# A fused adaLN block on one core: first-layer expert products issued in pairs on TensorE

## What is computed

```
h = layernorm(x) * (1 + ca) + sa
q, k, v = h @ Wq.T + bq, h @ Wk.T + bk, h @ Wv.T + bv      # 16 heads of 8
q = softmax(q, over the 8 channels of a head);  k = softmax(k, over the tokens)
state = k.T @ v (per head);  out = q @ state
x = x + ga * ((layernorm(out) * ln_g + ln_b) @ Wo.T + bo)
h = layernorm(x) * (1 + cb) + sb
logits = h @ router_w                                       # 8 experts, the top 2 are kept
y = sum over the chosen e: gate_e * (gelu(h @ w_in[e] + b_in[e]) @ w_out[e] + b_out[e])
x = x + gb * y
```

## Time and profile before

| | |
|---|---|
| median of 3 runs | 424.73 us (422.46 to 429.39) |
| the profiled execution | 429.81 us, its span 427.9 us |
| TensorE busy | 385.2 us of the span |
| VectorE, ScalarE, GpSimd busy | 302.7, 294.3, 221.0 us |
| mean granted TensorE clock | 0.954 of full speed |

### The profile page before, as it was taken

How to read it: one execution, slowest core, us unless ns; L and a number is a source line. 1 busy time by engine, 2 the same in 40 slices (tenths; PEclk the granted TensorE clock), 3 DMA queues, 4 the chain that set the end, 5 groups by cost and what they waited for, 6 DMA issues and landing times.

```text
span 427.9 us, 8780 instructions
## 1 busy us (share of the span) xinstructions
PE 385.2 (90%) x2660; PEld 347.4 (81%) x2660; DVE 302.7 (71%) x1080; ACT 294.3 (69%) x518; POOL 221.0 (52%) x222
## 2 busy tenths in 40 slices
PE   4545777999999999999999999999999999999895
PEld 3445575899888888898898988888989989989885
DVE  3576474678778787878887878878787876764631
ACT  3445547685786878695959778687869596776541
POOL 3432516245564747465556556473746555565341
PEclk9968666799999999999999999999999999999999
DMA  6721005042240606061432415050605132324060
GB/s 199 271 87 38 2 27 197 1 149 100 58 167 28 221 25 222 25 190 56 124 123 70 154 40 205 26 221 25 222 25 171 53 119 106 128 98 190 36 221 27
DMA packets 17789, 47.52 MB, mean 111 GB/s; under 512 B 2068, under 2 KB 4967, under 8 KB 17511
## 3 DMA queue, kind: packets, MB, share of 16 engines
q1 hardware_dynamic: 17568, 46.84, 31.6%
q10 hardware_dynamic: 198, 0.41, 0.3%
HBM read 42.76 MB, written 4.48 MB: 110 GB/s over the span
## 4 chain that ended last, share of the span: by engine, by line
PE 52%; DVE 17%; issue 10%; ACT 7%; POOL 4%; ACTq 1%; DVEq 0%; POOLq 0%
PE pY L647 19%; PE pH L635 6%; PE pH L636 5%; PE pH L637 5%; ACT u L468 3%; ACT L468 3%; DVE top L876 3%; PE pC L587 3%; DVE yg L907 2%; DVE qs L802 2%; DVE qmax L798 2%; PE pB L627 1%; DVE qs L793 1%; PE pB L614 1%; DVE lg_cut L882 1%
## 5 line engine op out<-in xcount | busy, mean ns | idle before, releaser
L647 PEld LDWEIGHTS pY<-wout,v 128*128 128x128 f32 x1024 | 126.4, 191 | 5.7
L647 PE MATMUL pY<-wout,v 128*128 128x128 f32 x1024 | 129.4, 275 | 0.0
L468 ACT ACTIVATE u<-pH,cols 128x512 f32<-128x512 f32 x128 | 87.1, 684 | 38.2 <-PE pH L637 38.0
L338 POOL TENSOR_TENSOR v<-u,gate_bc 128x512 f32<-128x512 f32 x48 | 67.0, 1397 | 48.8 <-ACT u L468 33.8
L902 DVE TENSOR_TENSOR v<-u,gate_bc 128x512 f32<-128x512 f32 x80 | 61.1, 766 | 26.9 <-ACT u L468 13.1
L635 PE MATMUL pH<-h_hi,win_hi 128*128 128x512 f32 x128 | 60.0, 469 | 9.4 <-ACT u L468 9.4
L636 PE MATMUL pH<-h_hi,win_lo 128*128 128x512 f32 x128 | 51.2, 400 | 0.0
L637 PE MATMUL pH<-h_lo,win_hi 128*128 128x512 f32 x128 | 50.7, 396 | 0.0
L328 POOL TENSOR_TENSOR rstd_o<-ve_o,neg_half 128x4 f32<-128x4 f32 x16 | 16.3, 1016 | 57.2 <-DVE ve_o L836 57.2
L346 POOL TENSOR_TENSOR h_lo<-h,h_hi 128x512 fp32r<-128x512 f32 x16 | 21.1, 1317 | 41.2 <-ACT h_hi L409 41.2
L436 ACT ACTIVATE eq<-qs 128x512 f32<-128x512 f32 x16 | 10.1, 631 | 38.7 <-DVE qs L802 38.7
(11 more groups left out here) (144 smaller groups left out, 881.9 us busy)
## 6 DMA issues: line engine op xcount, KB each, us to landing
gate_bc<-route_scratch SPq DMA_DIRECT2D x64, 512.0 KB, 5.4
x_all<-in_L_attn_x SPq DMA_DIRECT2D x16, 256.0 KB, 6.7
out<-x_all SPq DMA_DIRECT2D x16, 256.0 KB, 2.0
gates<-gate_scratch SPq DMA_DIRECT2D x1, 2048.0 KB, 6.9
gb_bc<-gb_scratch SPq DMA_DIRECT2D x1, 1024.0 KB, 4.8
win<-in_L_ffn_w_in SPq DMA_DIRECT2D x1, 512.0 KB
wout<-in_L_ffn_w_out SPq DMA_DIRECT2D x1, 512.0 KB
wmod_sb<-in_L_wmod ACTq DMA_DIRECT2D x1, 384.0 KB, 3.5
```

Source lines behind the costliest of these rows:

```text
L338: pool.tensor_tensor(v[:, e % U, :], u[:, e % U, :], gate_bc[:, par, e, :], ALU.mult).then_inc(s["vp_done"], 1)
L468: act.activation(u[:, e % U, :], pH[:, e % 2, :], ACT.Gelu_apprx_tanh, bias=cols[:, e:e + 1]).then_inc(s["gelu_done"], 1)
L647: i = mm(pY[:, t * P:(t + 1) * P], v[:, e % U, t * P:(t + 1) * P], wout[:, e, :], start=False, stop=(e == NE - 1), skip_group_check=True)
```

## The change

Only PE's `step` is changed, and in it only the order. Before, the eight first-layer products of a step stood apart, each with other PE work ahead of it. After, they stand in four pairs (0 and 1, 2 and 3, 4 and 5, 6 and 7), and the other PE work stands in the gaps. What hidden and combine do, which buffers they use and what they wait for is the same; so is the order on every other engine.

```diff
                 if M:
                     hidden(b, par, 0)
+                    hidden(b, par, 1)
                 if A1:
                     hT(b + 3)
                 if A2:
                     state(b + 2)
-                if M:
-                    hidden(b, par, 1)
                 if Y:
                     combine(b - 1, nxt, 5)
                 if B:
                     h2T(b + 1)
-                if M:
-                    hidden(b, par, 2)
                 if Y:
                     combine(b - 1, nxt, 6)
+                if M:
+                    hidden(b, par, 2)
+                    hidden(b, par, 3)
+                if Y:
                     combine(b - 1, nxt, 7)
                 if A1:
                     kT(b + 3)
-                if M:
-                    hidden(b, par, 3)
                 if A2:
                     attend(b + 2)
...
                 if M:
                     hidden(b, par, 4)
+                    hidden(b, par, 5)
...
                 if M:
                     combine(b, par, 0)
-                    hidden(b, par, 5)
                     combine(b, par, 1)
                     hidden(b, par, 6)
+                    hidden(b, par, 7)
                 if B:
                     gate_turn(b + 1)
                 if M:
                     combine(b, par, 2)
                     combine(b, par, 3)
-                    hidden(b, par, 7)
                     combine(b, par, 4)
```

More of the change, by code:

```diff
@@ L664, in step @@
                     h2T(b + 1)
+                if Y:
+                    combine(b - 1, nxt, 6)
                 if M:
                     hidden(b, par, 2)
+                    hidden(b, par, 3)
                 if Y:
-                    combine(b - 1, nxt, 6)
                     combine(b - 1, nxt, 7)
```

## The result

The changed kernel takes 460.5 us in the median (460.36 to 460.99, 4 runs) against 424.97 us before (422.46 to 429.39, 4 runs). The ratio is 1.082, 95% interval 1.077 to 1.087: slower by 8%, twice the 3.8% that was forecast, and 12 us above the upper end of the range. The profiled execution took 460.52 us, its span is 458.5 us. That of the kernel before is the slowest of its four (429.81 us), so the two traces differ by 30.7 us and the medians by 35.5.

The account below looks back on a forecast made before the run. Bound: PE's work from h6 to kT, then the VectorE and ScalarE chain to the next h6. Ten steps at 1.5 us (15.0), +1.6 for the step to b = 12, -0.5 at the start: +16.1 on 424.73, 440.8 us; range 433.5 to 448.5.

Parts of the forecast that it names:

- rival 3: TensorE's clock: 5 us behind h7 at 1.2 GHz, a step 5 us longer, about 495 us; chance 0.04.
- the term for the hold: VectorE's nmr waits for GpSimd's h2_low, so kT's 2.11 us delay lengthens a step by only 1.5 us.
- the 1.2 of the forecast: On GpSimd, h2_low was to move later in the step by some 1.2 to 1.4 us.
- its upper end: Hold between GpSimd's h2_low and VectorE's nmr stays in full: a step grows by 2.11 us, 448 us; chance 0.12.
- The ruler: PE work or a wait ahead of kT lengthens the step in full; behind kT there is slack under 1 us.
- -0.5 us: At b = 0, h3 fills part of kT's 1.71 us wait for h_lo and h7 hardly waits: -0.5 us.

Follow-up runs that it names:

- the run with the four passes: Changed kernel plus four 128x512 TensorE passes, whose results nobody reads, between hidden(6) and hidden(7): 451.64 us, ratio 1.059.

## Why the prediction was wrong, point by point

**Direction and place were right.** h7 waits for gelu 5 behind ln1_apply, 1.14 us by the idle record, and starts 2.10 us after h6 where 2.11 was forecast. h6 waits as well. gateT_evac waits for gate_turn (1.18 us at 217.49). kbmax and kshift swap the hold. Gelu 5 first removes 28 us: the wait of h7 is the main cause, shown by that run and by h7's move alone (+17.8 us).

**The step that failed most is rival 3's rejection.** "The clock stood at 1.00 through every 0.7 us wait, and the idle share stays under half of that of the start" argued from shorter waits to longer ones. The clock fell in eight steps of eleven, each fall held PE at 1.2 GHz for some 3.4 us, and such a step lost some 1.5 us, 12.6 us in all; the run with the four passes shows it by taking that away and leaving the warm step as it is. The rival had also been priced as one lump of 5 us in every step, which made it look unlike anything that could be mixed with the forecast; a smaller price on top of the forecast was the right case, with a far larger chance than 0.04.

**The second is the term for the hold, 1.5 us a step.** A warm step grew by 2.06. In the warm step above the weighing of expert 2 starts 16.89 us after h6, against 14.86 before. These 2.03 are made of four pieces, each rounded: GpSimd's queue starts 1.17 later (the 1.2 of the forecast), h_low is stretched by 0.47, kshift follows kbmax (0.19), and 0.19 more between nmr and the weighing. What causes the last is not shown. The two starts lie 0.26 us apart in the steady steps of every run where kshift takes 0.16, and 0.07 where it is held. The prediction had named the mechanism of the stretch through the rule of the Trainium skill, GPSIMD Engine Reference, section Key points, that instructions with two SBUF inputs and GpSimd contend, and had set the result, 2.11 a step, as its upper end. By the rule the stretch was to be expected: the weighing of expert 7 has two SBUF inputs and h_low newly meets it. The run with that weighing moved agrees, 1.28 us against 1.74. I kept the rule as a bound where the order already showed who would meet whom. Between kT of b = 1 and of b = 12 that run takes 273.3 us against the 278.0 with the four passes alone, so the stretch is worth 4.7 us.

**The ruler was only half right.** That all work ahead of kT lengthens the step in full fell with two runs: h3 alone costs 0.38 and not 0.70, and c7 taken away gives nothing. The chain from kT gets through kbmax and kshift only when GpSimd's queue is done. In the changed kernel the long way round (h7, q_turn, qT, ln2_apply, gelu 0, h_evac, h_low) carries the delay to GpSimd too, which is why next to nothing was absorbed.

**The start.** -0.5 us was forecast for b = 0; kT of b = 1 starts 2.4 us earlier (95.98 against 98.34). But the run with h2_low behind residual2, whose PE order is that of before, has it at 94.20. The traces tell these executions apart by the clock: from 70 to 80 us it averages 0.54 in the profile of before, and 1.00 in that of the changed kernel and in that run. The forecast had read "what it did at the low clock" off that one profile. So the difference is one between executions, and no run shows the -0.5.

**The sum against the traces.** Over the eleven steps from kT of b = 1 to kT of b = 12 the forecast had 16.6 us, and the traces show 34.0. Without the falls of the clock it would be 21.4 (278.0 less 256.6), so 4.8 us were missing in the term for the hold and 12.6 for the clock. The eleven steps agree with the difference of the medians (35.5) to 2 us only: against the 427.16 of before in the later runs it is 33.3. Nothing in the waits says why three of the steps stayed at 1.00, and that stays open. No run separates the length of the two waits from their distance; that the first wait matters is argued from one comparison, the run with h7's move alone. That the second is needed is shown twice: once the four passes fill it, or gelu 5 comes first, the wait of 1.3 us ahead of h6 stands alone and the clock stays up.

## What to carry to other kernels

Before instructions of one kind are put together on an engine, look at what the consumer has queued between the two answers that they need: with two buffers, the second of a pair waits for whatever stands between its two readers. Here one swap on ScalarE (gelu 5 ahead of ln1_apply) is worth 28 us, once the pairs are there. A new wait on TensorE of a microsecond close to another one had a second price here, in the clock; such a price belongs on top of the forecast, not beside it as an unlikely lump. Where a tiny VectorE operation takes a microsecond, read which GpSimd operation ends with it: the queue behind that operation may be the bound, and moving the operation may only move the hold.

## What the runs showed of the hardware

- With two waits on TensorE (1.3 and 1.14 us, 0.8 us of work between them) its granted clock fell from 1.00 to 0.50 in 8 of 11 steps; with 0.46 and 1.15 us in 3 of 11; with 1.36 and 0.20 us in none, nor with one wait of 1.3 us (gelu 5 first). The fall began 1.7 to 2.9 us after h6's start, in two of the eight steps during the second wait and in the others at its end or up to 0.8 us behind it, and the lower level lasted 3.4 us each time, though PE worked without a gap from 241.18 on in the step shown.
- Small VectorE operations with two SBUF inputs (kbmax, kshift, lshift; 0.16 to 0.19 us alone) ended with the GpSimd operation beside them, at up to 1.2 us. Between two GpSimd operations in a row one got through: before, kbmax ended with the weighing of expert 1 (240.90), and kshift, started at 240.94, was held by h2_low. Small ones with one input were held as well: before, the copy of top (243.83) took 1.09 us and ended with residual2, and ve (L773 at 236.88) took 1.28 and ended with h_low, against 0.17 us for ve in the run with h2_low between the weighings.
- Of two large ones the one that started second paid, in each pairing that I looked at. The weighing of expert 7 started at 224.45 and took 0.69 us, h_low at 224.55 and took 1.74. In the run with h2_low between the weighings, GpSimd's weighing of expert 5 started at 251.05 and took 1.28, qn at 251.62 and took 1.25; h_low at 236.16 took 1.27, a weighing at 236.27 took 1.72. This is read off the rows; no run was made for it.
